# Attention's beginning: stacks copied within SBUF, maxima over eight banks, normalising by halves

## The reference, cut to what matters

```python
x_h = x.reshape(b, t, h, d).transpose(0, 2, 1, 3)
xw = jnp.einsum('bhtd,hde->bhte', x_h, w_att_val)
att = jnp.einsum('bhte,bhse->bhts', xw, x_h) / jnp.sqrt(jnp.asarray(d, x.dtype))
att = jax.nn.softmax(att, axis=-1)
vx = x @ wv_w.T + wv_b
```

## Time and profile before

| | |
|---|---|
| median of the runs | 1489.31 us |
| profiled execution, its time | 1486.98 us |
| its span | 1485.1 us |
| PE busy | 1422.1 us (96%) |
| DVE busy | 1267.9 us (85%) |
| ACT busy | 866.0 us (58%) |
| POOL busy | 659.4 us (44%) |

### The profile page before, as it was taken

The page is one execution under the profiler, slowest core; times in us unless marked ns, Lnnn a source line. Parts: engine busy times, 40 slices in busy tenths (PEclk is TensorE's granted clock), DMA queues, the critical chain, the costliest instruction groups (busy, mean ns, idle before and its releaser), DMA issues. The chain is left out here.

```text
span 1485.1 us, 32215 instructions
## 1 busy us (share of the span) xinstructions
PE 1422.1 (96%) x8562; PEld 882.9 (59%) x8562; DVE 1267.9 (85%) x2644; ACT 866.0 (58%) x1730; POOL 659.4 (44%) x910
## 2 busy tenths in 40 slices
PE   4699999999999999999999998899999999999998
PEld 2345555555555555555555554577777777777776
DVE  5788888888888888888888887599999999999995
ACT  1477777777777777777777777533333333333332
POOL 2346446446446445445545523234343343434341
PEclk7799999999999999999999999999999999999999
DMA  7655455455456456356356353000000000000000
GB/s 209 192 157 161 133 155 162 124 160 167 122 157 173 119 154 178 111 159 182 106 163 169 103 150 90 1 15 15 18 14 18 14 18 14 18 14 18 14 18 22
DMA packets 99433, 148.09 MB, mean 100 GB/s; under 512 B 20928, under 2 KB 58176, under 8 KB 99392
## 3 DMA queue, kind: packets, MB, share of 16 engines
q1 hardware_dynamic: 82272, 137.08, 32.4%
q10 hardware_dynamic: 17120, 10.51, 2.8%
HBM read 85.02 MB, written 65.27 MB: 101 GB/s over the span
## 5 line engine op out<-in xcount | busy, mean ns | idle before, releaser
L1102 DVE TENSOR_REDUCE neg_max<-ring 128x1 f32<-128x512 f32 x1024 | 642.6, 682 | 107.0 <-PE ring L842 103.3
L991 ACT ACTIVATE probs<-scores 128x512 f32<-128x512 f32 x1024 | 531.2, 602 | 186.2 <-PE scores L853 175.8
L1552 PE MATMUL gu_bank<-splits,f_x_T 128*128 128x352 f32 x1024 | 313.7, 459 | 0.1
L842 PE MATMUL ring<-x_stack,q_stack 64*128 64x512 f32 x1024 | 233.9, 455 | 30.5 <-DVE neg_max L1102 18.8
L875 PE MATMUL ring<-probs,v_quad 128*32 128x512 f32 x2048 | 246.2, 598 | 4.2 <-DVE neg_max L1102 4.1
L1552 PEld LDWEIGHTS gu_bank<-splits,f_x_T 128*128 128x128 f32 x1024 | 189.6, 190 | 95.4 <-ACT f_x_T L1526 0.5
L850 PE MATMUL scores<-q_stack,x_stack 64*128 64x512 f32 x1024 | 206.4, 398 | 4.9 <-DMA max_stack<-max_rows 2.6
L842 PEld LDWEIGHTS ring<-x_stack,q_stack 64*128 64x128 f32 x1024 | 98.3, 188 | 185.7 <-DVE neg_max L1102 138.1
L853 PE MATMUL scores<-max_stack,max_ones 64*128 64x512 f32 x1024 | 203.0, 392 | 0.0
L1308 POOL TENSOR_TENSOR f_small<-f_small,eps 128x1 f32<-128x1 f32 x64 | 43.0, 672 | 295.8 <-DVE f_small L1275 295.8
L649 POOL TENSOR_TENSOR pv_rows<-pv_more,pv_rows 128x512 f32<-128x512 f32 x63 | 80.8, 1283 | 180.8 <-ACT pv_more L997 180.8
(11 more groups left out here) (129 smaller groups left out, 1981.5 us busy)
## 6 DMA issues: line engine op xcount, KB each, us to landing
x_rows<-splits SPq DMA_DIRECT2D x128, 256.0 KB, 3.3
x_stack<-x_rows SPq DMA_DIRECT2D x128, 256.0 KB, 4.0
q_stack<-q_rows SPq DMA_DIRECT2D x248, 128.0 KB, 4.0
q_rows<-splits SPq DMA_DIRECT2D x64, 256.0 KB, 2.2
out_dram<-x_all SPq DMA_DIRECT2D x64, 128.0 KB, 1.7
x_all<-in_L_attn_x_dram ACTq DMA_DIRECT2D x14, 512.0 KB, 4.1
w_raw<-slabs SPq DMA_DIRECT2D x14, 192.0 KB, 3.9
slabs_kept<-w_turned SPq DMA_DIRECT2D x14, 192.0 KB, 3.8
```

The lines of the kernel that those rows point to most:

```text
L842: pe.matmul(bank(tiles[m])[:, :], row_tile(q_stack[q], m)[:, p, s * P:(s + 1) * P], row_tile(x_stack[q], m)[:, p, :], start=True, stop=Tru ...
L991: act.activation(probs[j][:, k, :], scores[k][:, :], ACT.Exp).then_inc(p_ready, 1)
L1102: dve.tensor_reduce(neg_max[g % 2][:, at:at + 1], tile[:, :], AX.X, ALU.max, negate=True).then_inc(m_used, 1)
L1552: m = pe.matmul(gu_bank[c][:, :], x_T[u][:, a, :], gate_up_T[:, a, c * CH:(c + 1) * CH], start=(a == 0), stop=(a == HALVES - 1))
```

## The change

The stacks of quads 0 and 1 of batch 0 are no longer loaded from DRAM. `direct_stacks` copies one part of a head's 16 rows within SBUF, 16 partitions of 512 numbers (32 KB), so that one pair of a quad takes 16 DMAs, 64 in all. Of these, SP issues 12 and ACT 4 in `first_block` (pair 0 of quad 0), and in `attention_block` SP issues 16 and ACT 32 ahead of everything that was there. Half 0 of batch 0 is not stored to `x_rows` and `q_rows` any more. Each pair has a semaphore of its own, on which PE waits.

POOL's `half_read` waits until all 64 copies have landed, then fills the rest of `w_turned` and raises `stored[0]`, as the stores did. It stands ahead of the first `split_maxima`. The 16 tiles of quad 0 go through the four `ring` banks and the four `scores` banks in turn. x of batch 0 is normalised by halves, eight instructions instead of four, and PE transposes half 0 once its four are done. Half of the eight `qw` DMAs go from ACT's queue to SP's, ahead of `vw`. DVE's statistics of batch 1 stand earlier. SP loads quad 3 only after the first `max_stack` has landed.

```diff
+def direct_stacks(queue, g, p, k, stack, part, direct):
+    a = g * QUAD // HH
+    for m in range(ROWS):
+        h = g * QUAD % HH + PAIRS * m + p
+        queue.dma_start(row_tile(stack[g], m)[D * k:D * k + D, p, :].bitcast(F32), part[h:P:HH, a, :].bitcast(F32))\
+             .then_inc(direct, 16)
...
             load_x(0, 1, x_first)
+            sp.wait_ge(qw_zero, 1)
+            for k in range(HH // 2, HH):
+                load_qw(sp, k)
             sp.dma_start(vw[:, :, :], wv_w.rearrange("(n p) e -> p n e", p=P)).then_inc(vw_loaded, 16)
...
+            sp.wait_ge(xh_done, 1)
+            for k in (0, 3):
+                direct_stacks(sp, 0, 0, k, x_stack, xh, direct[0][0])
             sp.wait_ge(xl_done, 1)
-            store_parts(sp, 0, 0, x_rows, (xh, xl, xl, xh), stored)
+            for k in (1, 2):
+                direct_stacks(sp, 0, 0, k, x_stack, xl, direct[0][0])
             sp.wait_ge(ql_done, 1)
-            store_parts(sp, 0, 0, q_rows, (qh, ql), stored)
+            for k in (1, 3):
+                direct_stacks(sp, 0, 0, k, q_stack, ql, direct[0][0])
             sp.wait_ge(bias_loaded, 32)
-            sp.wait_ge(stored[0], STORES)
-            load_x_stack(sp, 0, 0, x_stack, x_rows, stack_loaded)
...
                 act.activation(qh[:, a, :], q_bank[a][:, :], ACT.Copy, scale=D ** -0.5).then_inc(qh_done, 1)
+                if a == 0:
+                    act.wait_ge(qh_done, 1)
+                    for k in (0, 2):
+                        direct_stacks(act, 0, 0, k, q_stack, qh, direct[0][0])
             move(1)
-            act.wait_ge(stored[0], STORES)
-            load_q_stack(act, 0, 0, q_stack, q_rows, stack_loaded)
...
-                pe.wait_ge(xn_done, TT)
+                pe.wait_ge(x_half_done if a == 0 else xn_done, TT)
...
+    def max_bank(c, q, k):
+        if isinstance(c, int) and c == 0 and q == 0:
+            return (*ring, *scores)[k % 8]
+        return bank(("max", (q - 2) % QUADS, k))
...
-            pool.memset(w_turned[:, :], 0.0).then_inc(w_stored, 16)
+            def half_read():
+                for g in range(DIRECT):
+                    for p in range(PAIRS):
+                        pool.wait_ge(direct[g][p], 2 * PARTS)
+                pool.memset(w_turned[:, P:], 0.0).then_inc(stored[0], STORES)
+            pool.memset(w_turned[:, 0:P], 0.0).then_inc(w_stored, 16)
             pool.wait_ge(pool_set, set_up())
+            half_read()
             split_maxima(0, 0, True)
...
-            load_x_stack(sp, 0, 1, x_stack, x_rows, stack_loaded)
+            direct_x(sp, 0, 1)
+            direct_x(sp, 1, 0)
             store_parts(sp, 0, 1, x_rows, (xh, xl, xl, xh), stored)
             store_parts(sp, 0, 1, q_rows, (qh, ql), stored)
-            for g in range(2, QUADS):
-                load_stacks(sp, 0, g, x_stack, q_stack, x_rows, q_rows, stored, stack_loaded)
+            load_stacks(sp, 0, 2, x_stack, q_stack, x_rows, q_rows, stored, stack_loaded)
             sp.wait_ge(max_loaded[0], 16 * ROWS)
+            load_stacks(sp, 0, 3, x_stack, q_stack, x_rows, q_rows, stored, stack_loaded)
             copy_weights()
...
-            load_q_stack(act, 0, 1, q_stack, q_rows, stack_loaded)
+            direct_q(act, 0, 1)
+            direct_q(act, 1, 0)
+            direct_q(act, 1, 1)
+            direct_x(act, 1, 1)
             store_maxima(0, 0)
             load_maxima(0, 0)
```

More of the change, by code:

```diff
@@ L132, in build @@
             with ExitStack() as ctx:
-                first_block(nc, ctx, x, w_att, wv_w, wv_b, out_w, out_b, **tiles)
+                first_block(nc, ctx, x, w_att, wv_w, wv_b, out_w, out_b, raw_x, **tiles)
             with ExitStack() as ctx:
@@ L286, in _ @@
             act.wait_ge(qw_zero, 1)
-            for k in range(HH):
-                act.dma_start(qw[k:P:HH, :, k * D:(k + 1) * D], w_att[k:H:HH].rearrange("a d e -> d a e"))\
-                   .then_inc(qw_loaded, 16)
+            for k in range(HH // 2):
+                load_qw(act, k)
             move(0)
@@ L333, in _, with statistics @@
         def _(dve):
-            def statistics(d):
+            def statistics(d, tiles):
                 wait(dve, mv_done, TT * d)
-                for s in range(TT):
+                for s in tiles:
                     dve.bn_stats(stats[:, s, :], x_all[:, d * TT + s:d * TT + s + 1, :]).then_inc(bn_done, 1)
@@ L351, in normalize, with normalize_half @@
                                rstd[:, s:s + 1]).then_inc(xn_done, 1)
+            def normalize_half(a, done):
+                dve.wait_ge(rstd_done, 1)
+                for s in range(TT):
+                    dve.tensor_scalar(xn[:, s, a * P:(a + 1) * P].rearrange("p (d h) -> p d h", h=HH),
+                                      x_all[:, s, a * P:(a + 1) * P].rearrange("p (h d) -> p d h", d=D),
+                                      mean_var[:, s, 0:1], rstd[:, s:s + 1], ALU.subtract, ALU.mult).then_inc(done, 1)
             def low_x(a):
@@ L366, in _ @@
             dve.wait_ge(x_first, 16)
-            statistics(0)
+            statistics(0, range(TT))
             aggregate(0)
-            normalize(0)
+            normalize_half(0, x_half_done)
+            normalize_half(1, xn_done)
             dve.wait_ge(qw_loaded, 16 * HH)
@@ L432, in attention_block @@
     x_loaded, ffn_loaded = sem("x_loaded"), sem("ffn_loaded")
-    STACK = ROWS * 3 * 16
+    direct = [[sems[f"direct{g}{p}"] for p in range(PAIRS)] for g in range(DIRECT)]
     pool_set, v_spread = sem("pool_set"), sem("v_spread")
@@ L583, in attention_block, with direct_x, direct_q @@
     COPIES = 12
+    def direct_x(queue, g, p):
+        for k, part in enumerate((xh, xl, xl, xh)):
+            direct_stacks(queue, g, p, k, x_stack, part, direct[g][p])
+    def direct_q(queue, g, p):
+        for k, part in enumerate((qh, ql, qh, ql)):
+            direct_stacks(queue, g, p, k, q_stack, part, direct[g][p])
     def head_of(place):
@@ L836, in max_scores @@
                 tiles = [("max", g, ROWS * n + m) for m in range(ROWS)]
[L837 to L840, removed]
+                if isinstance(c, int) and c == 0 and q < DIRECT:
+                    if s == 0:
+                        pe.wait_ge(direct[q][p], 2 * PARTS)
+                elif n == 0:
+                    pe.wait_ge(stack_loaded[q], loads_before(q, c))
+                if isinstance(c, int) and c == 0 and q == 0:
+                    wait(pe, m_used, ROWS * (n - 4) + ROWS)
+                else:
+                    for semaphore, count in room(tiles, b):
+                        pe.wait_ge(semaphore, count)
                 for m in range(ROWS):
-                    pe.matmul(bank(tiles[m])[:, :], row_tile(q_stack[q], m)[:, p, s * P:(s + 1) * P],
+                    pe.matmul(max_bank(c, q, ROWS * n + m)[:, :], row_tile(q_stack[q], m)[:, p, s * P:(s + 1) * P],
                               row_tile(x_stack[q], m)[:, p, :], start=True, stop=True).then_inc(m_ready, 1)
@@ L1099, in reduce_max @@
                 at = TT * (PAIRS * m + p) + s
-                tile = bank(("max", (g - 2) % QUADS, k))
+                tile = max_bank(0 if isinstance(i, int) and i == 0 else 1, g, k)
                 dve.wait_ge(m_ready, QUAD * TT * i + k + 1)
```

32 lines of the change are left out of this document (20 added, 12 removed).

## The result

The changed kernel takes 1497.3 us (median of 4 runs, 1496.76 to 1498.3) against 1488.52 us for the kernel before, timed beside it. The ratio is 1.006, with a 95% interval of 1.0045 to 1.0075: slower by 8.8 us, which is clear of noise. The forecast of 1487.5 us was wrong, and so was its range of 1482.4 to 1494.5. The profiled execution's span is 1494.7 us.

The account below looks back on a forecast made before the run. PE was busy for 96% of the span, so only the shift of the first scores counted. Border +0.7 us and border to first scores -2.55 us made -1.85 us, from 1489.31 to 1487.5 us; range 1482.4 to 1494.5.

Parts of the forecast that it names:

- The step that failed: ACT's queue after the blocks' border: 0.42 us per copy issue, bounds 0.27 and 0.66; last of 32 begins 13.0 us later.
- Landing: The direct copies within SBUF, from issue to landing: 2.1 us, bounds 1.7 and 4.
- S - T: From the blocks' border, where POOL begins the next block, to the first scores: 24.8 us before, 22.2 forecast, -2.55.
- S: Start of the first scores, which need max_stack: 46.31 us before; forecast 22.25 us after the blocks' border.
- The start: In first_block: vw late, xn at 9.8 us; four copies between the halves of q; border at 22.2, 0.7 us late.
- The eight banks: Quad 0's 16 tiles end 11.0 us after the border, 16.0 before; the gain goes in DVE's idling before its transpose.
- No stall at quad 0's second pair: Quad 0's second pair lands 5.2 us after the border, before DVE's eighth tile at 6.1; DVE isn't stalled.
- Dear issues: Rival: ACT's issues between border and maxima's store cost 0.66 us each; net +6.65 us, 1496; chance 0.13.
- The two queues hinder each other: Rival: SP's 16 issues hold up ACT's in full, last copy 6.7 us later; net +4.9, 1494.2; chance 0.06.
- Slow landing: Rival: copies behind SP's bulk stores land in 4 us, maxima's trip as before; +2.1 to +4, 1491.4 to 1493; chance 0.08.
- The clock: Rival: PE's shorter pause leaves full clock up to the first scores; 2.6 us more, net -4.5, 1484.9; chance 0.06.
- Cheap issues: Rival: ACT's copy issues cost 0.27 us each, the transpose follows DVE's own end; net -6.8 us, 1482.5; chance 0.17.

Follow-up runs that it names:

- copies_halved: The changed kernel with the last 8 x copies of quad 1 issued by SP instead of ACT, 24 on each queue; 1491.53 us, ratio to before 1.0028.
- qw_on_act: The changed kernel with all eight qw DMAs on ACT's queue again, so vw is SP's second issue; 1495.79 us, ratio to before 1.0062.
- ring_alone: The changed kernel with quad 0's maxima in the four banks of ring alone, as before; 1497.97 us, ratio to before 1.0076.
- before_eight: The kernel before with quad 0's maxima over eight banks; 1485.97 us, ratio to before 0.9989.
- copy_forms: The changed kernel with other copy shapes on ACT's queue and 20 more copies into scratch; its time says nothing, issues 0.64 to 0.68 us in six of seven forms.
- before_halves: The kernel before with x of batch 0 normalised by halves and batch 1's statistics earlier on DVE; 1488.41 us, ratio to before 1.0004.
- all_three: The changed kernel with qw's eight DMAs on ACT, the last 8 x copies on SP, half_read behind the first split_maxima; 1486.23 us, ratio to before 0.9985.
- eight_late3_halves: The kernel before with quad 0's maxima over eight banks, quad 3 loaded after the first max_stack, normalising by halves; 1485.3 us, ratio to before 0.9975.
- copy_forms_two: The changed kernel with 31 more DMAs to scratch on ACT's queue ahead of quad 1's copies; its time says nothing, issues from 0.50 to 1.19 us by form.

## Why the prediction was wrong, point by point

**The step that failed** is "I take 0.42 [...] bounds 0.27 and 0.66" for an issue, the term of 31 copies on ACT ahead of POOL's wait. The mechanism was as forecast: DVE stands at its transpose, released by POOL, and POOL by a DMA. But the last issue began 21.05 us after the border and not 13.1, that is +8.0. The mean from one start to the next is 0.68 (21.05 / 31), just above the upper bound, which was the price of `qw`, the only DMA of 16 partitions in the trace. Alone or beside SP's copies they took 0.64; from 34.8 to 38.3 us, beside SP's bulk stores, four issues took 0.9 us more than that. I took the price of a store that looked alike in its dimensions.

**Landing** was the second error: 5.35 us from the last copy's issue to POOL's fill instead of 2.1, +3.2, beyond the bound of 4. The common value was right (median 2.0); the last copy alone counted, and it was issued into SP's loads of quad 2, which began at 39.82. The copies issued at 38.9 and 39.6 still landed in 2.0 us, the six from 40.2 on in 4.1 to 5.2. copies_halved shows the same from the other side: 2.1 without the loads. By the sum, S - T is 22.25 + 8.0 + 3.2 = 33.45; measured were 32.67, because the way from the transpose to S took 5.45 and not 6.15 (ten tiles of quad 1 were the limit, as the floor of 5.6 said).

**The start** was right within 0.2 us. xn at 9.33 (9.8 forecast; `vw` landed 2.9 us after its issue, not 3.3), four copies between the halves of q 2.53 us (1.7 forecast), border 22.37 (22.2). The forecast's 17.65 for ACT is 17.58 by its own terms (15.9 + 4 x 0.42), which changes nothing. qw_on_act puts the price of `vw`'s place at 2.0 us of border.

**The eight banks** were right: their gain is lost in the changed kernel (ring_alone) and real where DVE's transpose isn't held (before_eight, 1.9 us of transpose).

**No stall at quad 0's second pair** was wrong. It was forecast to land at T + 5.2; PE waited 5.61 us for it and went on at T + 6.8. It cost nothing at the end, since DVE waited later anyhow. The forecast also put too few bytes on SP's loads: a quad's stack is two loads of 256 KB and four of 128 KB, 1.0 MB and not 768 KB, and two quads 2.0 MB; no term of the sum was worked out from it.

**The rivals.** *Dear issues* was the case, with its place and sign: 1496 us forecast, 1497.3 measured. I gave it 0.13 and left its far part, with 1496, out of the range, on the ground that `qw`'s pieces are small and that it stood at the very start. copy_forms shows that neither makes the difference. It also shows that the reason given for this rival, the 16 partitions, was not the right one, since 64 and 128 cost the same; that `qw`'s number fitted is in part luck. *The two queues hinder each other* fell for copies beside copies (copies_halved); beside the six bulk stores the 0.9 us above speak for a small part of it. *Slow landing* came true as an addition. *The clock* fell: half clock came at 23.9 us, PE had no matmul from 36.0 to 49.5, and full clock came at 58.1, went again at 61.5 and was back for good at 68.3, 13.3 us after S (12.7 before). *Cheap issues* fell. The quoted rule of the Trainium skill (Perfetto Trace Analysis, "DMA Instruction — HWDGE (DVE, Sync)"), a generator locked for one sequencer at a time, does not show in these runs at this rate: two queues side by side issue every 0.64 us each, as ACT does alone.

**From S to the end** the shift is kept, but not exactly. The start of the n-th exponential, changed minus before, is 8.6 us for the first, 6.4 for the 193rd, 7.3 for the 961st and 9.6 for the last. So a part is regained early and a part lost late, 1.5 us of it by a fall of the clock at 915 us (last section), and so the near agreement of 8.73 at S with 8.8 of the medians is partly luck.

## What to carry to other kernels

Price a row of small DMAs by the number of issues on the queue, and look at what else is queued on that engine: here 32 copies of 32 KB kept ACT's queue for 21.7 us, though the bytes were few. A DMA that resembles another in its dimensions need not cost the same, and the same DMA need not cost the same beside other traffic (0.373 and 0.60 us for one store); where the nearest rows run from 0.27 to 0.66 us and 31 issues hang on them, the range has to take in the dearest. And when a transfer on the chain is slow to land, first look for bulk loads issued just before it that nobody needs yet: delaying one of those brought S 2.9 us forward.

## What the runs showed of the hardware

Within SBUF an issue cost about the same whatever it moved, 0.64 to 0.68 us for 8 KB, 32 KB and 256 KB (copy_forms), except beside SP's bulk stores, where single issues took up to 1.07 us. The 16 KB store of the maxima with quad 3's loads beside it took 5.8 us to the issue that waits for it, and 2.1 us without them.

PE's clock gave way once more in the changed kernel's run, from 2.4 to 1.2 GHz at about 915 us, and was back before 920. The stretches (columns as in the earlier trace rows), of the changed kernel:

```profile
905.00:915.00 10.00, 7.04 (x52) 3.43 (x50) 7.20 (x13) 6.38 (x14) 4.04 (x8) 0.99 0.75 185
915.00:920.00 5.00, 5.00 (x30) 2.45 (x32) 2.69 (x5) 2.58 (x6) 0.25 (x2) 0.68 0.00 0
```

And of ring_alone at the same place of the program:

```profile
904.80:914.80 10.00, 7.12 (x52) 3.56 (x52) 7.14 (x13) 6.45 (x14) 4.00 (x9) 1.00 0.73 181
```

Between the 971st exponential and the 981st the shift against the kernel before goes from 8.1 to 9.5 us, and this is the fall; in ring_alone it stays at 7.7. Four other traces have the fall at this place (before_halves, all_three, eight_late3_halves, copy_forms_two), the other nine don't. PE's busy time ahead of it doesn't tell them apart: 7.04 of 10 us in the changed kernel and 7.44 in eight_late3_halves with the fall, 7.12 in ring_alone and 7.30 in copies_halved without. What sets it off is open, and with one trace of each kernel it isn't shown whether it belongs to a kernel or to an execution. It took about 1.5 us, enough to hide a gain of that size at the start.
